# Tap sums by TensorE matmuls in the setup, late key pieces' low halves on GpSimd, and the last image's layer 1 summed map by map

## The reference, cut to what matters

```python
t = cbs(x, cv1_w, cv1_bn, 0)              # x is the group-normalised input
ys = [t[:, :C], t[:, C:]]
for i in range(N):                        # N = 2 bottlenecks
    z = cbs(ys[-1], m_cv1_w[i], m_cv1_bn[i], 1)      # 3x3
    z = bot_attention(z, m_qkv_w[i], m_rw[i], m_rh[i])
    z = silu(bn_eval(conv2d(z, m_cv2_w[i], 0), m_cv2_bn[i]))
    ys.append(ys[-1] + z)
x = x + cbs(concatenate(ys), cv2_w, cv2_bn, 0)
...
s, t = argmax(softmax(S), 1), argmax(softmax(T), 1)
w_eff = conv * t_gain * (t[:, None] == s[None, :])
dense = conv2d(gn(x) * s_gain, w_eff);  p = argsort(t)
x = x + dense[:, p[p]]
```

## Time and profile before

| | us |
|---|---|
| median of 3 runs (3112.54 to 3113.22) | 3112.66 |
| the profiled execution, its own time | 3110.56 |
| its span, first to last instruction | 3108.4 |
| TensorE busy in the span | 2882.4 (93%) |
| VectorE, ScalarE, GpSimd busy | 1949.1, 1733.6, 1130.0 |

### The profile page before, as it was taken

One profiled execution on the slowest core, in us unless ns is written; L12 is line 12 of the kernel. 1 busy time (PEld: TensorE's weight loads), 2 busy tenths in 40 slices (PEclk: granted clock), 3 DMA queues, 4 the chain that ended last, 5 costly groups with the idle time before them and its releaser, 6 DMA issues.

```text
span 3108.4 us, 62540 instructions
## 1 busy us (share of the span) xinstructions
PE 2882.4 (93%) x27616; PEld 1580.7 (51%) x27616; DVE 1949.1 (63%) x2612; ACT 1733.6 (56%) x2176; POOL 1130.0 (36%) x790
## 2 busy tenths in 40 slices
PE   3699999999998999999999999999999999999997
PEld 2355454554555545654545545555456545465453
DVE  7676566756567465764657656674657656566564
ACT  3448383565646575383834747365654748438381
POOL 2235342443226261362523434153413616115151
PEclk7799999999999999999999999999999999999998
DMA  5110101101010010201002010100101001010001
GB/s 174 70 58 2 42 12 51 53 2 42 25 58 32 2 42 28 85 2 41 5 25 85 2 41 15 68 32 1 42 28 55 32 1 42 28 58 2 1 12 44
DMA packets 35902, 111.98 MB, mean 36 GB/s; under 512 B 12976, under 2 KB 15024, under 8 KB 32944
## 3 DMA queue, kind: packets, MB, share of 16 engines
q1 hardware_dynamic: 35632, 107.98, 9.7%
HBM read 85.69 MB, written 22.28 MB: 35 GB/s over the span
## 4 chain that ended last, share of the span: by engine, by line
PE 71%; ACT 11%; DVE 10%; issue 3%; POOL 3%; DMA 1%; SPq 0%; POOLq 0%; DVEq 0%
PE ps_u L856 39%; PE ps_u L1027 10%; PE ps_u L870 7%; DVE row_max L1471 4%; PE ps_o L1048 4%; PE ps_u L1001 3%; ACT wide L1224 3%; PE ps_o L1049 3%; ACT ps_u L1224 3%; PE ps_o L1050 3%; POOL y_rest L1604 1%; ACT probs L1228 1%; DVE wide L1245 1%; POOL z L1604 1%; ACT qk L1203 1%
## 5 line engine op out<-in xcount | busy, mean ns | idle before, releaser
L1471 DVE TENSOR_REDUCE row_max<-ps_u 128x2 f32<-128x1024 f32 x512 | 618.0, 1221 | 225.9 <-PE ps_u L1001 225.9
L1626 POOL TENSOR_TENSOR probs<-wide,probs 128x1024 f16<-128x1024 f32 x256 | 544.9, 2129 | 171.0 <-ACT probs L1228 160.4
L1093 ACT ACTIVATE wide<-ps_u,par_t 128x512 f32<-128x512 f32 x224 | 173.6, 775 | 537.8 <-PE ps_u L856 498.0
L1027 PE MATMUL ps_u<-qk 64*128 64x512 f16 x3072 | 418.7, 378 | 44.1 <-ACT wide L1224 20.3
L1048 PEld LDWEIGHTS ps_o<-v_ext,probs 128*128 128x128 f16 x4096 | 374.9, 96 | 161.5 <-issue 129.0
L1048 PE MATMUL ps_o<-v_ext,probs 128*128 128x65 f16 x4096 | 431.7, 193 | 0.9
L1049 PE MATMUL ps_o<-v_ext,probs 128*128 128x64 f16 x4096 | 429.1, 195 | 0.0
L1050 PE MATMUL ps_o<-v_ext,probs 128*128 128x65 f16 x4096 | 426.5, 191 | 0.0
L856 PE MATMUL ps_u<-y_pad,w_c 128*128 128x512 f16 x1728 | 394.1, 383 | 0.0
L1049 PEld LDWEIGHTS ps_o<-v_ext,probs 128*128 128x128 f16 x4096 | 380.5, 97 | 6.2
L1245 DVE SCALAR_TENSOR_TENSOR wide<-wide 128x512 f32<-128x512 f32 x256 | 176.6, 692 | 328.2 <-ACT wide L1094 310.4
(11 more groups left out here) (209 smaller groups left out, 4394.6 us busy)
## 6 DMA issues: line engine op xcount, KB each, us to landing
w_c<-w_c_dram SPq DMA_DIRECT2D x7, 3072.0 KB, 9.9
w_c<-w_c_dram SPq DMA_DIRECT2D x8, 2304.0 KB, 8.8
xn<-in_x_dram SPq DMA_DIRECT2D x32, 512.0 KB, 6.0
o_nat<-in_x_dram SPq DMA_DIRECT2D x64, 256.0 KB, 2.7
out_dram<-qk SPq DMA_DIRECT2D x32, 512.0 KB, 2.6
probs<-in_L_conv_m_cv_w_dram SPq DMA_DIRECT2D x3, 1152.0 KB, 8.7
w_c_dram<-w_c SPq DMA_DIRECT2D x1, 3072.0 KB, 9.8
w_c_dram<-w_c SPq DMA_DIRECT2D x1, 2304.0 KB, 7.9
```

The source lines that it names most:

```text
L1027: ins = e.matmul(ps_u[:, use.slot + q, :], lhsT, rhs, start=k == 0, stop=k == 3)
L1471: e.reduce_max(row_max[:, g % 2, :, it, half], ps_u[:, use.slot:use.slot + 2, :], axis=AX.X).then_inc(*dve_max.up(i, b, g, half, it))
L1626: e.tensor_tensor(p_part(s, 1), wide[:, w.slot, :], p_part(s, 0), ALU.subtract).then_inc(*pool_lo.up("p", i, b, s))
```

## The change

It has three parts.

1. Setup. The tap sums of g4 and g5 are made by TensorE: instead of 24 transposes a group, each plane is a float32 product with an identity or a minus identity, one such matmul for the first two planes and three accumulating ones for the last two, so eight a bank. GpSimd's four instructions a group go. From g3 on, every second bank's low half goes to GpSimd (`on_pool`), with an extra ScalarE copy into `wide`: 13 of 28 banks. `l1_rows` works in PSUM, in two banks by turns, without the copy and with one ScalarE pass, and its low half becomes a step of its own, `l1_lo`, one group later. `l1_keys` stands ahead of g1's scale, `l1_masks` ahead of g3's banks, each `l1_rows` one group earlier, `l1_unit` ahead of g8, and the scaling of g4 and g5 behind the banks of the group before.
2. Attention. The pieces `("k", 0, 1)` and `("k", 1, 1)` of all 16 bottlenecks join `ON_POOL`. In first bottlenecks `m1_split(1, 1)` stands ahead of value piece 0.
3. Last image. Six of the eight `l1` tiles are begun together: the matmuls of input tile 0 for all six, then 1, then 2, then tile by tile those of input tile 3; the last two tiles follow as before.

```diff
+        def on_pool(g, k):
+            return g >= 3 and k % 2 == 1
...
             for k, bank in enumerate(banks_of(GROUPS[g])):
-                plan("w_bank", g, k, bank, setup_ring.take(("act_cast", ("w", g, k)), ("dve_lo", ("w", g, k))))
+                use, w = setup_ring.take(("act_cast", ("w", g, k)), *([] if on_pool(g, k) else [("dve_lo", ("w", g, k))])), None
+                if on_pool(g, k):
+                    w = wide_ring.take(("pool_lo", ("w", g, k)))
+                plan("w_bank", g, k, bank, use, w)
...
                 if g == 2:
                     plan("l1_ranks")
-                if g == 3:
                     plan("l1_masks")
                 if 4 <= g < 4 + CT:
-                    plan("l1_rows", g - 4)
+                    plan("l1_lo", g - 4)
+                if 3 <= g < 3 + CT:
+                    plan("l1_rows", g - 3)
...
+                if g == 7:
+                    plan("l1_unit")
...
-            plan("l1_unit")
...
-        ON_POOL = ("q", 0, 1), ("q", 1, 1), ("v", 0), ("v", 1), ("v", 2), ("v", 3)
+        ON_POOL = ("q", 0, 1), ("q", 1, 1), ("k", 0, 1), ("k", 1, 1), ("v", 0), ("v", 1), ("v", 2), ("v", 3)
...
+            first = []
+            if i + 1 == B:
+                first = [(m, n, banks.take(0.0, 20.0, ("dve_x1", ("l1", i, m, n)))) for m in range(CT - 1) for n in range(2)]
+            for t in range(CT - 1):
+                for m, n, use in first:
+                    plan("l1", i, m, n, use, t, t + 1)
...
                             if by_plane(g):
-                                cols, (dy, unit_at) = slice(q // UNITS * P, (q // UNITS + 1) * P), divmod(q % UNITS, PLANES)
-                                w = src[:, m, cols, 3 * dy + 2 * unit_at] if unit_at < 2 else tap_sums[:, g % 2, unit_at - 2, cols, dy]
+                                cols, (dy, plane_at) = slice(q // UNITS * P, (q // UNITS + 1) * P), divmod(q % UNITS, PLANES)
+                                w0, w1, w2 = (src[:, m, cols, 3 * dy + dx] for dx in range(3))
+                                once(pool_small, "minus_ident")
+                                if plane_at < 2:
+                                    ins = products(o, [((w0, minus_ident), (w2, ident[:, :]))[plane_at]])
+                                else:
+                                    ins = products(o, [(w0, ident[:, :]), (w2, ident[:, :]), (w1, (ident[:, :], minus_ident)[plane_at - 2])])
...
                 elif kind == "l1_unit":
-                    e.wait_ge(*act_cast.at("w_l1", CT - 1, 0))
+                    once(dve_small, "l1_split", CT - 2)
+                    once(dve_small, "l1_split", CT - 1)
...
                     dst, src = w_bank(g, bank, use, 0)
+                    if w:
+                        until_free(e, w)
+                        e.activation(as_bank(g, bank, wide[:, w.slot, :]), src, ACT.Copy)
                     e.activation(dst, src, ACT.Copy).then_inc(*act_cast.up("w", g, k))
...
-                    e.activation(wf, wf, ACT.Copy, scale=f).then_inc(*act_cast.up("l1_scaled", m))
-                    e.wait_ge(*act_cast.now())
-                    e.activation(v_split[:, m, 0, :], wf, ACT.Copy).then_inc(*act_cast.up("l1_hi", m))
+                    e.activation(v_split[:, m, 0, :], ps_o[:, m % 2, :], ACT.Copy, scale=row_l1[:, m % 2, 3:4]).then_inc(*act_cast.up("l1_hi", m))
```

More of the change, by code:

```diff
@@ L358, in setup_plan @@
                 plan_group_banks(g)
-                if g + 1 < len(GROUPS) and not by_plane(g + 1):
+                if g + 1 < len(GROUPS):
                     plan("w_apply", g + 1)
@@ L585, in plan_bottleneck @@
                 m1_silu(1, 1)
+                m1_split(1, 1)
                 piece("v", 0)
                 next(maxima)
-                m1_split(1, 1)
                 piece("v", 1)
@@ L755, in plan_image @@
             sums = planes_ahead(i + 1, new_maps) if i + 1 < B else iter(())
+            first = []
[4 more added lines that the diff above has]
+                    plan("l1", i, m, n, use, t, t + 1)
             for m in range(CT):
                 for n in range(2):
-                    plan("l1", i, m, n, banks.take(2.6, 1.0, ("dve_x1", ("l1", i, m, n))))
+                    if first:
+                        plan("l1", i, *first.pop(0), CT - 1, CT)
+                    else:
+                        plan("l1", i, m, n, banks.take(2.6, 1.0, ("dve_x1", ("l1", i, m, n))), 0, CT)
                     if m < HT:
@@ L915, in tensor @@
                     once(dve_small, "l1_split", CT - 1)
+                    once(dve_small, "l1_unit")
                     for j in range(2):
@@ L935, in tensor @@
                 elif kind == "setup_end":
-                    for k in range(len(banks_of(GROUPS[-1]))):
-                        once(act_cast, "w", len(GROUPS) - 1, k)
-                        once(dve_lo, "w", len(GROUPS) - 1, k)
+                    g = len(GROUPS) - 1
+                    for k in range(len(banks_of(GROUPS[g]))):
+                        once(act_cast, "w", g, k)
+                        once(*((pool_lo,) if on_pool(g, k) else (dve_lo,)), "w", g, k)
                 elif kind == "gn_mean":
@@ L1017, in tensor @@
                     once(pool_lo if ("q", pair, n) in ON_POOL else dve_lo, "q", i, b, pair, n)
-                    once(dve_lo, "k", i, b, pair, jt // 4)
+                    once(pool_lo if ("k", pair, jt // 4) in ON_POOL else dve_lo, "k", i, b, pair, jt // 4)
                     once(act_copy, "shift", i, b, g)
@@ L1078, in tensor @@
                 elif kind == "l1":
-                    i, m, n, use = a
-                    for t in range(CT):
+                    i, m, n, use, begin, end = a
+                    for t in range(begin, end):
                         once(dve_lo, "norm", i, 1, t)
-                    until_free(use)
-                    pairs = [p for k in range(CT) for p in three(lambda j: w_l1[:, j, k, m * P:(m + 1) * P], lambda j: x1_parts[:, k, j, HH[n]])]
-                    products(ps_u[:, use.slot, :], pairs).then_inc(*u_full.up("l1", i, m, n))
+                    if begin == 0:
+                        until_free(use)
+                    pairs = [p for k in range(begin, end) for p in three(lambda j: w_l1[:, j, k, m * P:(m + 1) * P], lambda j: x1_parts[:, k, j, HH[n]])]
+                    ins = products(ps_u[:, use.slot, :], pairs, start=begin == 0, stop=end == CT)
+                    if end == CT:
+                        ins.then_inc(*u_full.up("l1", i, m, n))
         def scalar(e):
@@ L1108, in scalar @@
                 if kind == "w_bank":
-                    g, k, bank, use = a
+                    g, k, bank, use, w = a
                     if by_plane(g) and not by_plane(g - 1) and k == 0:
@@ L1284, in vector @@
                 elif kind == "w_bank":
-                    g, k, bank, use = a
+                    g, k, bank, use, w = a
+                    if w:
+                        continue
                     e.wait_ge(*act_cast.at("w", g, k))
@@ L1524, in vector @@
                 elif kind == "l1":
-                    i, m, n, use = a
+                    i, m, n, use, begin, end = a
+                    if end < CT:
+                        continue
                     e.wait_ge(*u_full.at("l1", i, m, n))
```

82 lines of the change are left out of this document (43 added, 39 removed).

## The result

The changed kernel takes 3134.94 us (median of 4 runs, 3134.5 to 3135.48) against 3112.6 of the kernel before: a ratio of 1.0074, 95% interval 1.0061 to 1.0087. The forecast was 3112.3, the range ended at 3120, and 3137 had been named for rival E with a chance of 0.07.

A forecast was written before the change was run, and what follows sets the result against it. TensorE, busy 93% of the span, was taken as the bound outside the setup and the last image's end; -6.8 + 2.7 + 3.7 = -0.4 on 3110.56 gave 3110.2, with the median 2.1 above it 3112.3 us, range 3103 to 3120.

The forecast's parts named there:

- rival E: Setup, tap matmuls at the low clock: two groups and `l1_rows` 1 take 25 us more, 3137 us; chance 0.07.
- The step that failed: Setup, tap banks of g4 and g5: 16 records in steps of 0.114 us, 1.8 us a bank, 10.9 a group.
- The term of part 1: Setup up to the first `cv1` matmul: +2.7 us, bounds -3.0 to +6.
- The rest of the setup: Setup outside the taps: start 3.7 us earlier, later masks 2.45 us each, `l1_rows` 0 at 72.9, `l1_unit` 7.5 us.
- Part 2: Key pieces in the bottlenecks: 0.43 us lost in a second, 0.0 in a first; +3.7 us, bounds -4 to +11.
- rival B: Bottlenecks: VectorE's relief counts and ScalarE's copy hides behind TensorE; -4.0 instead of +3.7, 3104.6 us; chance 0.13.
- Part 3: Last image's end: matmuls start at 3074.2 instead of 3081.03 and never wait again; -6.8 us, bounds -7.0 to -3.4.

The follow-up runs named there:

- the run of the key pieces: The kernel before with only the late key pieces' low halves on GpSimd and the m1 split moved: 3117.53 us against 3111.33 (1.0020).

## Why the prediction was wrong, step by step

**The step that failed** is the sentence "A tap bank has eight matmuls, 16 records, 1.8 us", with "in steps of 0.114" ahead of it. The steps came from the earlier trace rows, float32 matmuls whose operands lie adjacent in SBUF; the new ones read every ninth element. Measured: 0.239 a record, 3.82 us a bank, 22.9 us a group at a clock of 1.00. Two groups are 24 us more than the sum had, the load of g8 comes 23.1 us late for it, and the run with adjacent weights takes all of it away. The term of part 1 was +2.7; at the first image's convolution it measured +25.0 (172.2 to 197.2 us) and with adjacent weights +1.7 (173.9).

What made the step look safe: half of the old transposes read the same weights nine apart, the other half the tap sums three apart, all at 0.115 each, and the trace's other transposes, of adjacent elements, were hardly faster (16 in 1.91 us). For transposes that is right (0.115 and 0.110), and it doesn't carry over to true matmuls, where one record seems to hold two passes over the operand (at 512 columns it lasts 0.430 us, and a whole float16 matmul of 512 columns lasts 0.216, 2.59 for 12); that it does isn't shown. The rows had no true float32 matmul with gaps, so the cost was unknown, and the bounds of part 1 should have held it; -3.0 to +6 left no room for a step of twice the length, 24 us.

**Rival E** gave 3137 and was off by 2, by luck: its cause was a low clock, and the windows show 1.00. (Its sum also slipped: two groups of 22.6 us are 23.4 over the forecast's, and `l1_rows` 1 at the low clock 3.6 more, 27 and not 25.) The Trainium skill's factor (TensorE: Matmul & The Clock Gate, Terms) gave 22 us a group too. The runs show a factor of 2.0 for adjacent operands (0.223 to 0.110 us) and 4.2 nine apart (0.478 to 0.115), so the figure held here only with the gaps. I had set it aside by the count of records, which doesn't tell how long a record lasts. The page that bears on the cause is another: SBUF — State Buffer, in Specifications (TRN2), speaks of lines of 16 bytes and asks for two reads in a line for the full rate. True float32 matmuls agree: 0.111 and 0.117 us a record at distances of 1 and 2 elements of four bytes, 0.175 at 3, and 0.233 at 4. Other reads don't: transposes nine apart take 0.115 for 0.110, and the stationary operand of a float16 matmul nine apart 0.063 for 0.055. So the rule doesn't tell which reads pay, and that the lines are the mechanism is argued from the place where the price stops growing, not shown.

**The rest of the setup** held: start 3.9 us earlier for 3.7 (the copy at 18.54), the three later masks 2.25 to 2.35 us each beside GpSimd for 2.45, `l1_rows` 0 at 71.37 for 72.9, one-column matmuls 6.96 us for 7.5, g8's transposes 3.65 for 3.8.

**Part 2** was right in mechanism and too small: +3.7 forecast, 7.1 measured. "First bottleneck: 0.3 is gained and about 0.3 lost again" is what the run of the key pieces shows up to the first `logits` (TensorE's key piece (0, 1) 0.29 us earlier, `logits` 0.01 late). In a second bottleneck `logits` is 0.30 us late (743.19 to 769.54, against 735.27 to 761.32 at value piece 2), not 0.43. What was missing comes behind: the maxima start 0.2 us later still, since `max` waited for the high half, and TensorE's query piece behind the first `logits` waits 0.19 us for one of them, in both bottlenecks. It is in the row at 770.77 above. About 30 us further on, each bottleneck loses another 0.1, whose cause I didn't follow. Together 0.3 in a first and 0.6 in a second bottleneck, 0.9 an image, where the prediction had 0.45. VectorE's relief didn't make up for it, as the prediction said against rival B.

**Part 3**: -6.8 forecast, -6.85 in the changed kernel's trace, -7.05 by itself.

With the failed step repaired (adjacent weights) the span is 2.5 us over that of the kernel before, where the forecast's sum was -0.4: 1.7 of the setup for 2.7, 7.4 of the attention for 3.7, and -6.7 of the end.

## What to carry to other kernels

Before an elementwise job goes to TensorE as a float32 matmul, look at how far apart the elements of its operands lie: a transpose that reads them at full speed says nothing about a true matmul. When a shift is to be found, follow one recurring instruction through both traces before reading shares: it splits the time by stage in one view. In a queue that works in order, put a load that something waits for ahead of a store that nobody waits for.

## What the runs showed of the hardware

At the full clock a transpose of 128x128 float32 leaves one record and takes 0.110 us from adjacent elements and 0.115 from elements nine apart. A true float32 matmul leaves two; with adjacent operands a record takes 0.106 us at 1 moving column, 0.111 at 128, 0.219 at 256 and 0.430 at 512; in these runs the load of the stationary operand costs nothing beside 128 columns or more. With either operand nine apart it takes 0.23 to 0.25 at 128. With adjacent operands a float32 matmul of two records so costs four times a float16 one: 0.223 to 0.055 us at 128 columns, 0.86 to 0.216 at 512. Float16 matmuls take 0.055 us adjacent, 0.063 with the stationary operand nine apart, and 0.246 with the moving operand nine apart. This last I had not expected: with the moving operand nine apart a float16 matmul lasts as long as a float32 record (0.246 and 0.237), though adjacent it lasts half as long. Why stays open, as does why transposes and float16's stationary operand hardly pay.
